# GpSimd's order in six stages of a two-layer transformer kernel: the MLP residual's bias goes first, another bias and a weight's gating go behind the first subtraction

## What is computed

```python
# layer 0 (16 heads of 16 channels, windows of 128 tokens, HID = 1024)
h = ln(x) * (1 + sc_msa) + sh_msa;  x = x + self_attn(h) * g_msa
h = ln(x) * (1 + sc_mca) + sh_mca;  x = x + topk_cross_attn(h, context) * g_mca
h = ln(x) * (1 + sc_mlp) + sh_mlp
u = h @ w_m1 + b_m1;                a, b = halves(u)
x = x + ((silu(a) * b) @ w_m2 + b_m2) * g_mlp
# topk_cross_attn: scores over 64 keys, top_k(16), softmax over these 16, weighted sum of values
# layer 1: x = x + (softmax(q k) v) @ Wp + bp, q from an adaptive layer norm of x
```

## Time and profile before

| what | value |
|---|---|
| device time, median of 3 runs | 1042.36 us |
| lowest and highest of the 3 | 1040.95, 1043.43 us |
| the profiled execution: device time | 1045.08 us |
| the profiled execution: span | 1042.9 us |
| busy share of the span: PE, DVE, ACT, POOL | 86%, 74%, 46%, 21% |

### The profile page before, as it was taken

One profiled execution on the slowest core, in us unless ns is written; L12 is line 12 of the kernel. 1 busy time (PEld: TensorE's weight loads), 2 busy tenths in 40 slices (PEclk: granted clock), 3 DMA queues, 4 the chain that ended last, 5 costly groups with the idle time before them and its releaser, 6 DMA issues.

```text
span 1042.9 us, 22090 instructions
## 1 busy us (share of the span) xinstructions
PE 899.7 (86%) x8088; PEld 654.4 (63%) x8088; DVE 776.9 (74%) x3953; ACT 475.2 (46%) x792; POOL 218.9 (21%) x162
## 2 busy tenths in 40 slices
PE   6987654998999989998999989998999898767985
PEld 4754542786667756785667765775777666644763
DVE  3647876997689966997599868996699758875322
ACT  3426313635574264625563456526462554315313
POOL 1015311412041213202041405120230403120010
PEclk9989686999999999999999999999999999988989
DMA  8250010000100102000100111000100110000000
GB/s 326 94 167 12 2 42 0 17 2 2 40 18 1 52 3 72 16 1 3 41 17 1 52 35 44 11 2 1 57 2 1 53 31 1 2 1 1 21 1 21
DMA packets 29051, 32.96 MB, mean 32 GB/s; under 512 B 4320, under 2 KB 26000, under 8 KB 28688
## 3 DMA queue, kind: packets, MB, share of 16 engines
q1 hardware_dynamic: 28944, 31.55, 9.3%
HBM read 25.19 MB, written 6.36 MB: 30 GB/s over the span
## 4 chain that ended last, share of the span: by engine, by line
PE 55%; DVE 33%; ACT 5%; issue 4%; DMA 1%; POOL 1%; SPq 0%; DVEq 0%; ACTq 0%; POOLq 0%
PE bank L1314 50%; DVE left L1062 9%; DVE top L1060 7%; DVE negm L1025 3%; DVE arena L1079 3%; DVE xh L973 3%; PE bank L1481 3%; DVE negm L1087 2%; PE bank L1332 2%; ACT arena L816 2%; DVE arena L1054 2%; DVE h_low L1072 1%; DVE vpad L1016 1%; ACT hT L705 1%; DMA w_m<-in_w_ada 1%
## 5 line engine op out<-in xcount | busy, mean ns | idle before, releaser
L1314 PE MATMUL bank<-w_m,arena 128*128 128x256 f32 x512 | 114.9, 386 | 6.1 <-issue 6.1
L601 POOL TENSOR_SCALAR veps<-mv 128x4 f32<-128x4 f32 (+1 forms) x33 | 8.1, 245 | 501.9 <-DVE mv L968 501.8
L1314 PEld LDWEIGHTS bank<-w_m,arena 128*128 128x128 f32 x512 | 98.5, 194 | 21.0 <-issue 7.2
L630 POOL TENSOR_TENSOR eS<-arena,top 128x1024 f32<-128x1024 f32 x32 | 61.9, 1934 | 228.4 <-DVE top L1060 228.4
L1062 DVE MATCH_REPLACE8 left<-top,arena 128x64 f32<-128x64 f32 x512 | 100.0, 213 | 0.0
L1062 DVE MATCH_REPLACE8 left<-top,left 128x64 f32<-128x64 f32 x512 | 99.9, 211 | 0.0
L759 ACT ACTIVATE arena<-bank 128x512 f32<-128x512 f32 x128 | 66.1, 603 | 60.1 <-PE bank L1314 60.1
L805 ACT ACTIVATE rden<-bank,chan 128x512 f32<-128x512 f32 x64 | 44.1, 688 | 102.7 <-PE bank L1314 74.0
L1314 PE MATMUL bank<-qr,w_m 128*128 128x512 f32 x256 | 82.3, 402 | 4.3 <-ACT qr L715 3.2
L1025 DVE TENSOR_REDUCE negm<-bank 128x4 f32<-128x512 f32 x128 | 78.8, 686 | 2.4 <-PE bank L1314 2.2
L1314 PE MATMUL bank<-qr,m_low 128*128 128x512 f32 x256 | 80.4, 396 | 0.0
(11 more groups left out here) (133 smaller groups left out, 1885.9 us busy)
## 6 DMA issues: line engine op xcount, KB each, us to landing
w_m<-in_w_m SPq DMA_DIRECT2D x4, 1024.0 KB, 5.6
xin<-in_x SPq DMA_DIRECT2D x4, 512.0 KB, 3.9
arena<-in_w_m SPq DMA_DIRECT2D x1, 2048.0 KB, 12.5
out<-x SPq DMA_DIRECT2D x4, 512.0 KB, 2.9
arena<-in_w_ada SPq DMA_DIRECT2D x1, 1536.0 KB, 11.1
gate<-gate_rows SPq DMA_DIRECT2D x12, 128.0 KB, 3.7
gated_bias<-gate_rows SPq DMA_DIRECT2D x12, 128.0 KB, 3.9
xin<-in_x SPq DMA_DIRECT2D x4, 384.0 KB, 3.1
```

Of the source, the lines that this page charges most:

```text
L630: nc.gpsimd.tensor_tensor(eS[:], S[:, t, :].rearrange("p (h n) -> p h n", h=H), top[:, :, 0:1].to_broadcast([P, H, LC]), ALU.subtract).the ...
L1314: return nc.tensor.matmul(dst, lhsT, rhs, start=start, stop=stop)
```

## The change

In each of the six full halves the order of GpSimd's instructions is changed; no instruction is added or taken away, and the programs of the other engines and of the DMA queue are the same. Before, GpSimd did after the two `layer_rstd`: bias 1, bias 2, (odd halves: gating of `w_co`), the first subtraction, bias 3, (even halves: gating of `w_so`). Now it does: bias 3, bias 1, the first subtraction, bias 2, and then the gating, in odd and even halves alike. The opening and closing stages are as they were.

```diff
                 layer_rstd(1, a)
                 layer_rstd(3, b)
+                add_bias(3, b)
                 add_bias(1, a)
+                subtract_max(c, 0)
                 add_bias(2, c)
                 if a % BLKS:
                     gate_weight(1, batch)
-                subtract_max(c, 0)
-                add_bias(3, b)
-                if a % BLKS == 0:
+                else:
                     gate_weight(0, batch)
                 subtract_max(c, 1)
                 subtract_max(c, 2)
```

## The result

The changed kernel takes 1040.08 us in the median of 20 runs (1035.55 to 1044.06), the kernel before 1046.31 us in 20 runs beside it (1038.39 to 1052.58). The ratio is 0.9951, with a 95% interval of 0.993 to 0.9971: 5.1 us faster, 3.0 to 7.3. (The two medians lie 6.2 us apart; gains are told by the ratio here.) Forecast were 2.9 us less and a time of 1039.5 us. The time was met to 0.6 us, but with luck: it was reckoned from the first three runs of before, whose median of 1042.36 lies 4.0 us under that of the 20, and the gain was set too low at the same time.

What follows compares the result with a forecast made beforehand. Up to `vpad` TensorE bounds even halves and VectorE odd ones; from there to the end of `mlp_in`, VectorE both. 2.1 us at `vpad` plus 0.8 for the clock made 2.9 off 1042.36: 1039.5 us, range 1037.4 to 1041.9.

Steps and rivals of the forecast that it cites:

- Where the time is: Full halves up to `vpad`: TensorE bounds even halves, VectorE odd ones; of 21.7 us VectorE time saved, 2.1 count.
- Rival (E): All of VectorE's normalisation saving counts: 21.7 us, 1020.7; chance 0.04, including everything between this and the forecast.
- The normalisation's price: VectorE's four L973 in `normalise(3, b)` fall to 1.39 us, from 5.48 in odd and 4.53 in even halves.
- The gain at `vpad`: Odd halves: `vpad` starts earlier, TensorE's wait behind `mlp_in` falls to 1.06 us; 2.1 us over three halves.
- The subtraction, bias 2 and the gating at nothing: GpSimd's reordered instructions end before their readers need them: worth 0; gating ends 1.0 us before `h_low`.
- Rival (C): GpSimd's gating meets `h_low` and delays VectorE's chain six times: 7.9 us against the 2.1 gain, so 1048; chance 0.05.
- Rival (D): VectorE's replacements wait until GpSimd is done, so `vpad` comes some 4.2 us late: about 1067; chance 0.02.
- The clock: TensorE's low clock behind the longer wait at a = 3 may vanish: 0 to 1.62 us, 0.8 taken.
- no low clock in the middle of the span: Expected sign in the changed profile: TensorE's granted clock shows no low stretch in mid-span; no size of its own.

Runs made afterwards that it cites:

- e1: New GpSimd order in the odd full halves only, old order in the even ones; ratio 0.9954 to the kernel before.
- e2: New GpSimd order in the even full halves only, old order in the odd ones; ratio 0.9995 to the kernel before.
- e9: Against the kernel before, only bias 2 and the gating moved last, bias 1 left beside the normalisation, bias 3 behind the subtraction; ratio 0.9971 to the kernel before.
- e3: Changed kernel, but the first subtraction left behind bias 2 and, in odd halves, the gating; ratio 0.995 to the kernel before.
- e11: The kernel before, unedited, run a third time; ratio 1.0007 to the kernel before.
- e6: The changed kernel, unedited, run again; ratio 0.9951 to the kernel before.
- e5: The kernel before, unedited, run again; ratio 0.998 to the kernel before.
- e7: The changed kernel with one more VectorE instruction of 0.7 us in each full half, beside the first chunk's `gated_linear`; ratio 1.0069 to the kernel before.

## Why the prediction was right, point by point

- **Where the time is.** "Up to `vpad` the even half is bound by TensorE and the odd half by VectorE": shown by e1 and e2. The even halves gave nothing, and the 21.7 us of the normalisation's excess brought only a few us of gain. (VectorE's 26.3 us less are these and, for the rest, mostly instructions that became a few ns shorter: the median replacement went from 211 to 208 ns, which is 3 us over 1024 of them.) Rival (E) is gone.
- **The normalisation's price.** 1.38 us, forecast 1.39, in five halves, and 1.45 at a = 4. That VectorE got on only between GpSimd's instructions is shown by the number of GpSimd instructions beside it: none 1.38, one bias 2.48 (e9), two 4.53, two and the gating 5.48.
- **The gain at `vpad`.** VectorE's idle time of 1.48 us was forecast at about 1.5, and TensorE's wait of 1.06 in odd halves came out at 1.03 to 1.05. The term of 2.1 us measured 3 x (113.72 - 112.97) = 2.3 us. The mechanism was right here, and not only the number.
- **The subtraction, bias 2 and the gating at nothing.** Shown by e3 for the subtraction. For the gating the cover is thin, as said: 1.2 us in the changed kernel, and 0.2 us per half lost once it is gone (e9). Rival (C) has its mechanism confirmed, and its condition was not met.
- **Rival (D).** The replacements would have had to wait for GpSimd. They don't: at most 218 ns in the changed kernel, with GpSimd busy beside half of them, and 226 before.

```profile
L1062 DVE MATCH_VALUE_LOAD left<-top,arena x512: 71/80/94, 88.7 to 921.5; 128x8 f32 x171
L1062 DVE MATCH_REPLACE8 left<-top,arena x512: 197/208/218, 88.8 to 921.6; 128x64 f32<-128x64 f32 x171
```

The prediction's way to this rival had a wrong step. It took a replacement for an instruction with two inputs in SBUF; these rows show two instructions, one that loads the eight maxima (128x8) and one with a single input of 128x64. So the replacements say nothing against the rule on two inputs in SBUF of the Trainium skill, "SBUF — State Buffer", section "SBUF: two separate sides". `h_low`, which reads `xh` and `qr`, bears it out: 889 ns where the gating's end meets it (e9, a = 2), 684 otherwise. The normalisation has one large input, and its price stands on the rows of this case alone.
- **The clock.** This is the term that was mis-sized. I took 0.8 us, half of one low stretch in one profile. The counts give more: 5 of 18 long waits, about 0.83 in three odd halves, at 1.55 us each, 1.3 us; with the four profiles that have the old order in all odd halves alone 4 of 12, 1.6 us. The granted clocks of the timed runs give 0.9 to 1.2. That makes 2.3 + 0.9 to 1.6 = 3.2 to 3.9 us. The profiles' middle stretches, three of before with 682.3 us in the mean and two of the changed kernel with 678.4, are 3.9 apart too; but about 1.0 of that is low stretches behind `mlp_in`, and some 0.6 are other events that fell unevenly, such as a low stretch at 90 us and a late store at a = 7 of e11. The forecast doubted this term because the profiled execution lay 2.7 us above the median of three runs; it lies below the median of 20. Its sign "no low clock in the middle of the span" failed: the changed kernel's profile has one, at a = 5, in the other place.
- **What is left.** The timed ratio says 5.1 us, with 3.0 to 7.3, so 3.2 to 3.9 is inside it and the forecast's 2.9 just outside. The remaining 1.2 to 1.9 us are not settled. Unedited copies of the kernel before came out at 0.998 and 1.0007, so one ratio scatters by as much; but the four kernels with the new order in odd halves (changed, e1, e3, e6) all lie between 0.995 and 0.9954.
- **The time itself.** 1039.5 against 1040.08 is luck in part. From the median of 20 runs of before, 1046.31, the same forecast would have been 1043.4, with a range of 1041.4 to 1045.9.

## What to carry to other kernels

An engine's saved time counts up to the next place at which it waits for another: look for an idle time, however small, that the other engine ends (0.15 us ahead of `vpad` told that the even halves would give nothing), and compare the periods of otherwise equal stages. Where such a change leaves idle time on an engine that is the bound a little later, move a piece of its later work into it; here that gave about 3.5 us on top of the change's 5.1. And where several GpSimd instructions that nobody needs soon stand in a row beside VectorE's normalisation of data in SBUF, they go behind it; one of them may stay if VectorE has to wait afterwards anyway, as in e9.

## What the runs showed of the hardware

- A GpSimd instruction beside VectorE's normalisation of 128x256 tiles makes one tile last up to 2453 ns instead of about 407. In the kernel before, the four tiles of an odd half took 1510, 2451, 1356 and 400 ns: one beside each GpSimd instruction, and the last alone. Beside MAX8 and MATCH_REPLACE8 it changes nothing: 170 MAX8 that ran wholly beside one took 210 ns in the median and the others 209, with 231 at most in that kernel; the replacements took 226 at most before and 218 in the changed kernel.
- TensorE's idle time behind `mlp_in` was followed by the lower clock in none of 60 halves when it was 1.26 us or less, and in 5 of 18 when it was 1.70 to 1.82 us; it then cost 1.5 to 1.6 us. One more VectorE instruction of 0.67 us per half made the kernel 12 us slower (e7), of which 4.0 are VectorE's chain and most of the rest goes with 13 us more at the lower level.
- The lower level also came in another place, behind waits of 0.69 and 0.77 us for ScalarE, in 12 of 78 halves, and cost 1.1 to 1.4 us each where nothing else befell the half.
- The stages ahead of the first full half are the same code in all kernels, and end between 170.7 and 178.4 us in the 13 profiles, with 44 to 58 us of it at the lower clock. That is a scatter of twice the change's effect, so total spans of single profiles can't tell it. The lengths of halves with the clock up can: equal halves mostly agree to 0.1 us, with single ones 0.2 to 0.3 off (113.97 at a = 5 of e5).
